# Laying a transposed attention mask into PSUM with ScalarE copies instead of identity matmuls, in the third phase of a four-layer cross-attention kernel

## What is computed

```
def _L3_xattn_ref(values, keys, queries, mask, w_out, b_out):
    # HEADS = 16, HEAD_DIM = 16, EMBED = 256
    energy = jnp.einsum('nqhd,nkhd->nhqk', q, k)
    energy = jnp.where(mask == 0, jnp.float32(-1e+20), energy)
    attn = jax.nn.softmax(energy / math.sqrt(EMBED), axis=3)
    out = jnp.einsum('nhql,nlhd->nqhd', attn, v).reshape(N, q_len, HEADS * HEAD_DIM)
    return out @ w_out.T + b_out
x = x + jnp.tanh(g_xattn[3]) * _L3_xattn_ref(ctx_1024, ctx_1024, _layernorm(x, axis=-1), mask_1x1xSxS2_ik0, ...)
```

## Time and profile before

| what | before |
|---|---|
| median of three runs | 4302.57 us |
| lowest and highest run | 4301.93 and 4303.57 us |
| profiled execution, from its first to its last instruction | 4135.2 us |
| median less that span | 167.4 us |
| PE busy, share of the span | 3911.6 us, 95% |
| DVE busy | 2263.8 us, 55% |
| ACT busy | 1747.7 us, 42% |
| mean granted clock of TensorE | 0.991 |

### The profile page before, as it was taken

The page is one execution under the profiler, slowest core; times in us unless marked ns, Lnnn a source line. Parts: engine busy times, 40 slices in busy tenths (PEclk is TensorE's granted clock), DMA queues, the critical chain, the costliest instruction groups (busy, mean ns, idle before and its releaser), DMA issues. The chain is left out here.

```text
span 4135.2 us, 77612 instructions
## 1 busy us (share of the span) xinstructions
PE 3911.6 (95%) x28960; PEld 2760.0 (67%) x28960; DVE 2263.8 (55%) x6853; ACT 1747.7 (42%) x3685; POOL 1067.4 (26%) x1239
## 2 busy tenths in 40 slices
PE   7999999999999999999998989999899999889998
PEld 4666666666666666666665549997666666459965
DVE  4556555655565565556555542123677777544445
ACT  4455545554544555455455221111354454414420
POOL 2222221222222122212221001111112232245667
PEclk9999999999999999999999999999999999999999
DMA  3003113303321330233031027995112221139954
GB/s 119 1 14 120 59 65 118 120 11 110 120 84 40 118 120 28 94 120 110 17 113 62 26 78 273 330 334 204 29 58 72 78 88 50 54 136 332 337 180 150
DMA packets 285453, 472.85 MB, mean 114 GB/s; under 512 B 23008, under 2 KB 224608, under 8 KB 276512
## 3 DMA queue, kind: packets, MB, share of 16 engines
q1 hardware_dynamic: 227632, 371.88, 26.4%
q0 software_dynamic: 24480, 66.88, 5.3%
q10 hardware_dynamic: 32976, 29.13, 2.0%
HBM read 266.74 MB, written 201.06 MB: 113 GB/s over the span
## 5 line engine op out<-in xcount | busy, mean ns | idle before, releaser
L488 POOL TENSOR_SCALAR a_wide_p<-a_wide_p,a_w_inv 128x512 f32<-128x512 f32 x512 | 355.3, 706 | 1427.5 <-DVE a_w_inv L1149 1427.5
L923 ACT ACTIVATE a_wide_p<-a_wide_p,a_row_min 128x512 f32<-128x512 f32 x512 | 363.6, 713 | 143.5 <-DVE a_row_min L1144 143.4
L1219 DVE TENSOR_REDUCE a_q_pad<-ring 128x4 f32<-128x1024 f32 x256 | 301.0, 1218 | 76.7 <-PE ring L712 76.7
L1144 DVE CUSTOM_DVE_ANT_0 a_wide_p<-ring,a_neg_keys 128x512 f32<-128x512 f32 x387 | 256.4, 688 | 135.8 <-PE ring L572 135.7
L572 PE MATMUL ring<-a_qk 64*128 64x512 f32 x774 | 288.3, 642 | 10.7 <-DVE a_wide_pt L1154 4.0
L980 ACT ACTIVATE a_probs<-ring 128x1024 f32<-128x1024 f32 x256 | 250.6, 1019 | 72.7 <-PE ring L726 72.7
L1669 PE MATMUL ring<-b_xgt,b_we 128*128 128x128 f32 x2016 | 235.6, 275 | 0.8 <-DVE b_xgt L1859 0.5
L2783 DVE CUSTOM_DVE_ANT_0 shared_w<-ring,c_neg_mask 128x256 f32<-128x256 f32 x512 | 186.5, 421 | 90.8 <-PE ring L2346 90.8
L1669 PEld LDWEIGHTS ring<-b_xgt,b_we 128*128 128x128 f32 x2016 | 230.2, 192 | 1.3 <-DVE b_xgt L1859 0.7
L2592 ACT ACTIVATE c_probs<-ring 128x1024 f32<-128x1024 f32 x128 | 130.9, 1023 | 177.5 <-PE ring L2338 177.4
L551 PE MATMUL acc<-a_kv_t,shared_w 128*128 128x512 f32 x392 | 191.5, 611 | 1.2 <-ACT a_kv_t L914 1.2
(11 more groups left out here) (456 smaller groups left out, 8600.0 us busy)
## 6 DMA issues: line engine op xcount, KB each, us to landing
d_cells<-a_neg_keys SPq DMA_DIRECT2D x66, 2048.0 KB, 16.5
b_we<-in_experts SPq DMA_DIRECT2D x63, 1536.0 KB, 9.0
d_we<-in_experts SPq DMA_DIRECT2D x159, 256.0 KB
d_results<-d_yb ACTq DMA_DIRECT2D x159, 128.0 KB
a_k_t<-in_ctx_keys SPq DMA_DIRECT2D x16, 512.0 KB
a_v_pad<-in_ctx_values SPq DMA_DIRECT2D x16, 512.0 KB
c_k_t<-in_ctx_keys SPq DMA_DIRECT2D x16, 512.0 KB, 3.8
c_v_pad<-in_ctx_values SPq DMA_DIRECT2D x16, 512.0 KB, 3.6
```

What stands on the lines that cost most here:

```text
L488: ins = pool.tensor_scalar(wide_p[:, h % 4, t, :], wide_p[:, h % 4, t, :], w_inv[:, t, h:h + 1], 1.0, ALU.mult, ALU.mult)
L923: ins = act.activation(wide_p[:, h % 4, t, :], wide_p[:, h % 4, t, :], ACT.Exp, scale=-1.0, bias=row_min[:, h, t:t + 1], accum_out=row_sum ...
L1144: dve.tensor_tensor_reduce(wide_p[:, h % 4, t, :], wbank(name), neg_keys[w % 2][:], -0.125, 3.0e38, ALU.add, ALU.min, row_min[:, h, t:t + ...
L1219: dve.tensor_reduce(q_pad[:, :, 2 * i:2 * i + 2, HD].rearrange("p t h -> p h t"), s, AX.X, ALU.max, negate=True).then_inc(nr.taken(name), 1)
```

## The change

ScalarE puts the mask into the by-key slot for steps 1 to 7: behind each exponential but the last it waits for its own exponential to be done, and copies `neg_mask_t`, the 512 columns twice over, into the 1024 columns of `tbank`. PE waits for the copy (`mask_laid`) and issues no mask matmuls in these steps; its score matmuls accumulate onto what ScalarE wrote. Step 0 keeps its two mask matmuls.

```
@@ n_scores, TensorE
                                 tr.wait_room(pe, ("T", tb, i))
-                                for j in range(2):
+                                if i:
+                                    pe.wait_ge(mask_laid, 7 * tb + i)
+                                for j in range(2 * (i == 0)):
                                     pe.matmul(tbank[:, 512 * j:512 * j + 512], ident_bf[:], neg_mask_t[:].rearrange("p k n -> p (k n)"),
                                               start=True, stop=False, skip_group_check=True)
@@ n_exps, ScalarE
                             act.activation(probs[:, s % 4, :, :, :].rearrange("p j k n -> p (j k n)"), tbank, ACT.Exp,
                                            scale=D ** -0.5).then_inc(tr.taken(name), 1)
+                            if s < 7:
+                                lay_mask(b, s + 1)
+
+                        def lay_mask(b, s):
+
+                            if (b, s) == (0, 1):
+                                gr.wait_taken(act, ("mask",))
+                            tr.wait_taken(act, ("T", b, s - 1))
+                            act.activation(tbank.rearrange("p (j n) -> p j n", j=2),
+                                           neg_mask_t[:].rearrange("p k n -> p (k n)").unsqueeze(1).to_broadcast([P, 2, 512]), ACT.Copy).then_inc(mask_laid, 1)
```

More of the change, by code:

```diff
@@ L2022, in build @@
                     weights_used = sem(ctx, "c_weights_used")
+                    mask_laid = sem(ctx, "c_mask_laid")
                     x_loaded = sem(ctx, "c_x_loaded")
```

## The result

| what | before | after |
|---|---|---|
| median of 20 runs, taken together | 4302.83 us | 4316.15 us |
| lowest and highest | 4299.15 and 4316.59 us | 4305.31 and 4325.01 us |
| ratio to before, 95% interval | | 1.0026 [1.0018, 1.0033] |

The changed kernel is 0.26% slower, some 11 us by the ratio. The forecast was 4301 us and no change. 4316 lies inside the range, but the interval leaves out no change.

What follows compares the result with a forecast made beforehand. PE was taken to set the pace, busy 41.9 of 43.5 us a turn. Turns 1 to 12 at -4.1, then +0.7, -1.0 and +2.0, made -2.4, taken as -2: from 4302.6 to 4300.6, said as 4301 us; range 4287 to 4320.

Steps and rivals of the forecast that it cites:

- the mask is laid at exponential + 2.14: By-key steps 1 to 7: exponential 1.02, own wait 0.04, copy 1.02 and release 0.06 us until PE starts.
- 68 intervals: Intervals between steps, over all turns, said to be set by the copy; each 0.1 us more costs 7 us.
- T1: By-key step 1 of a full turn, a long step: gain 0.43 us.
- T2: By-key step 2, a long step: gain 0.43 us, with 0.21 given back because exponential 2 has a lower bound.
- T5: By-key step 5, a long step: gain 0.43 us, nothing waiting within a microsecond on ScalarE's work behind the copy.
- T4: By-key step 4: scores from exponential 3 + 2.35 to + 2.14, gain 0.21 us.
- T7: By-key step 7: exponential 6, queued behind the copy and other ScalarE work, comes late; 0.93 us lost, all on the path.
- The sum: Shifts of all by-key steps in one full turn added: -0.34 us a turn, -4.1 over turns 1 to 12.
- a shift passes on whole: Third phase's end, behind PE's chain and a barrier: the summed shift, taken as -2 us, reaches the total time in full.
- T6: By-key step 6, a short step: 0.02 us lost.
- The rival that came out slower: ScalarE becomes the bound: chain of exponential, own wait, copy, release longer than 2.14; 4310 to 4320 us; chance 0.29.
- The 167.4 us: Distance of the runs' median above the profiled span, added to a span of about 4133 to forecast the time.

Runs made afterwards that it cites:

- without scatters: Third phase's router row scatters of blocks 0 to 14, and the waits for them, left out: kernel before 4161.23 us (0.9730), changed kernel 4202.48 us (0.9832).
- first profile: Profile of the unchanged kernel before, shown with the prediction: span 4135.2 us, from the kind of chip where before takes 4139 to 4140 us.
- second group: Runs on one chip: before 4304.64 us, changed 4311.10, changed with ScalarE's f_hidden queue moved 4312.32, copy ahead of steps 1, 2, 5 alone 4278.15.
- third group: Runs on one chip: before 4274.33 us, changed 4288.67; with the third phase's router row scatters left out, before 4161.23, changed 4202.48.
- copy and matmuls together: Changed kernel with PE's two mask matmuls issued again behind the wait for ScalarE's copy: 4225.18 us, 1.0207 of before.

## Why the prediction was wrong

- **Copy.** Forecast 1.02 us, measured 1.028. The Trainium skill's price (ScalarE: Activation LUTs, What ACT_TABLE_LOAD costs) gave 1.04; the trace agrees about as well with it. The prediction's "below 1 us higher" by that price is a slip: 0.02 x 68 is 1.4 us. The Trainium skill (PSUM — Partial Sum Buffer, Specifications) has ScalarE faster to PSUM than to SBUF. That is not seen here: this copy from SBUF to PSUM takes 1.028, the one of the same width from PSUM to SBUF 1.025. The two differ in their source too, so that this settles little. The own wait of 0.04 was right (copy at exponential + 1.05).
- **"the mask is laid at exponential + 2.14"**: mis-sized. From the copy's end to the first score matmul it takes 0.15 instead of 0.06, so scores start at + 2.23, and a short step is 3.40 instead of 3.30, 0.10 lost in place of 0.02. By the forecast's own price (68 intervals) this is 6 us. The 0.06 was read between an exponential and a mask matmul, another kind of matmul.
- **T1, T2, T5**: -0.43 with 0.2 given back, measured -0.43, -0.22 and -0.56. The last holds 0.13 that T4 had been given: T4 was forecast at -0.21 and shows 0.00, since exponential 4 waits for ScalarE's other work.
- **T7 late**: exponential 6 at + 4.42 forecast, + 4.46 measured; 0.93 lost forecast, 1.02 measured. The queue was read rightly.
- **The sum**: forecast -0.34 a turn. The one turn of 4 to 12 with a full clock, turn 5 without scatters, has -0.08 in all: 0.08 is missing at step 3, 0.08 at steps 4 and 5 together, 0.10 at 6 and 7. That turn 3 has -0.31 up to exponential 7 is luck: there T2 keeps its whole 0.43, since exponential 2 isn't held back yet, which makes up for the rest.
- **The last turns**, without scatters and up to each exponential 7: turn 13 has +1.1 instead of +0.7, and turns 14 and 15 have 0.0 instead of -0.5 each. Turn 16 has the forecast's +2.0 by exponential 5 and then 3.8 more, with the clock at its lower level.
- **The step that failed** is "a shift passes on whole", and with it the whole sum at a constant clock. The forecast itself said that "PE's busy time in the phase falls while its idle time rises", and gave that no price. I called the removed matmuls something that has "been standing in that wait's place". They also kept PE busy there: ahead of scores 3 its stop goes from 0.98 to 1.77 us at an unchanged pace, and each fall of the clock behind it costs 1.3 to 1.8 us. Behind the late T7 and the stop ahead of T6 the clock falls as well, and there a fall costs 1.7 us or more. In the turns 4 to 12 without scatters this is the whole 14.6 us: nine times -0.08 and some 15.3 for eight falls. The rival that came out slower had the right side and a small part of the mechanism: the chain is 0.09 longer than 2.14, in its release. Copy and own wait weren't dear, and the clock was not in it.
- **The 167.4 us** do not lie "around the instructions". They are the difference between two chips. Between the first profile (span 4135.2) and that of before in the second group (4300.8), 85.6 us arise in the turns 4 to 12, 29.0 in the turns 13 to 16, 47.8 behind the phase's last exponential and 3.2 ahead of turn 4. Without the scatters the first two are gone, and 22 us behind the phase with them. So I worked out steps for turns that, on the chip of the runs, last 49 to 58 us and not 43.5.
- The measured 0.26% is thus a mixture: losses of clock in the turns, made up in part in the turns with the stall, and a part outside the turns whose cause is open.

Not tried: the changed kernel with its scatters on a chip where before takes 4139. By the third group it should lose some 40 us there; that is an inference. Nor was the stop ahead of scores 3 filled with matmuls that nobody uses, which would test the stop by itself. The copy ahead of the steps 1, 2 and 5 alone is faster than both kernels on both kinds of chip, 0.9977 [0.9967, 0.9987] and 0.9946 [0.9925, 0.9967].

## What to carry to other kernels

Work moved to another engine gains nothing in a step where its result comes there no earlier than before. (Left out altogether, the mask gave 0.54 us in a short step.) On TensorE such a move can lose, since the stop grows and the clock may fall behind it. So list each step's stop before and after, and move work off TensorE only where the step is long. And where the profiled span and the runs' median are far apart, find out why before summing anything: here it was another chip, with another turn.

## What the runs showed of the hardware

- The granted clock fell to its lower level behind a stop of 1.77 us ahead of scores 3 in some turns and not in others with the same rows (turn 6 against turn 5 above), behind two stops of 0.89 and 0.96 us 4.4 us apart, and in three turns behind the 0.89 alone. Behind 1.62 us ahead of step 3 it stayed full in the turns 2 to 12 of copy and matmuls together. A fall costs 1.3 to 1.8 us a turn, and 3.2 where the lower level stays twice as long (turns 8 and 11 of the changed kernel without scatters). The Trainium skill tells of the like (TensorE: Matmul & The Clock Gate, A second HAM failure mode: psum-queue depth-cycling): short idles between groups of matmuls, while PSUM banks are cycled, make the clock go to and fro. The runs here agree, with stops of 0.89 to 1.77 us and a clock that goes between 1.00 and 0.50.
- In the traces of two chips (before takes 4306 and 4278 us there) PE's results reached ScalarE and VectorE late, once a turn, and only with the row scatters in the program: in turn 4 of before on the first, exponential 5 starts 5.7 us behind the recorded end of its scores. Exponential 5 is at + 5.6 without the scatters and at + 7.6 to + 12.7 with them (before, turns 4 to 12); on one chip where it takes 4139 us the same scatters leave the turn at 43.46. Missing records don't explain it: turn 4 of the third group's before has 377 matmul records with the scatters and 377 without, and with them PE stands still for 4.11 us. Whether it is the memory, the queue or something else stays open.
